# A metaformer kernel: token rows kept as fp16 halves and turned by transposing DMAs, a deeper split-ahead of the weights, and one product set for both embeddings

## What is computed

```
x = x + attention(ln_c(x))          # e1 = relu(w1 x + b1), e2 = relu(w2 x + b2), both with D = 64 channels
                                    # scores = e1^T e2, softmax; out = x attn; y = alpha * out + relu(w3 x + b3)
t = t + moe(ln_t(t))                # rmsnorm, router with 16 experts, top 4 of them per token
    gu = x @ gate_up_proj[e]        # (512 -> 2 * 1024), h = silu(gate) * up
    routed += aff * (h @ down_proj[e])   # (1024 -> 512)
    shared = (silu(x @ sgate) * (x @ sup)) @ sdown
x = x + scan(ln_c(x))               # 16 rows forward and back, one 512 x 512 matrix
t = t + ternary_ffn(ln_t(t))        # weights rounded to -1, 0, 1
```

## Time and profile before

| | before |
|---|---|
| median of 3 runs | 1105.28 us |
| lowest and highest | 1102.9 and 1105.73 us |
| the profiled execution's own time | 1101.8 us |
| span of its trace | 1100.1 us |
| mean granted TensorE clock | 0.957 of full speed |

### The profile page before, as it was taken

One profiled execution on the slowest core, in us unless ns is written; L12 is line 12 of the kernel. 1 busy time (PEld: TensorE's weight loads), 2 busy tenths in 40 slices (PEclk: granted clock), 3 DMA queues, 4 the chain that ended last, 5 costly groups with the idle time before them and its releaser, 6 DMA issues. The chain is left out here.

```text
span 1100.1 us, 21748 instructions
## 1 busy us (share of the span) xinstructions
PE 995.5 (90%) x8016; PEld 648.9 (59%) x8017; DVE 704.6 (64%) x1340; ACT 545.3 (50%) x898; POOL 150.1 (14%) x159
## 2 busy tenths in 40 slices
PE   5977499899899999999999999999998997985796
PEld 3434444367566666766667766766674446872453
DVE  5378896465666556576566665665764886658774
ACT  4623544255565455565555655565654413233674
POOL 0030001101011012011102210120112640002000
PEclk9998599899999999999999999999998998996998
DMA  8601134435656555556546764664567640000001
GB/s 304 232 1 38 40 131 161 140 115 189 217 186 207 171 176 200 176 199 215 186 142 225 234 209 149 238 219 168 204 229 224 194 114 1 1 0 0 1 20 57
DMA packets 116438, 162.68 MB, mean 148 GB/s; under 512 B 7569, under 2 KB 85393, under 8 KB 116402
## 3 DMA queue, kind: packets, MB, share of 16 engines
q1 hardware_dynamic: 104530, 130.30, 35.2%
q0 software_dynamic: 9168, 30.02, 8.1%
q10 hardware_dynamic: 2704, 1.87, 0.5%
HBM read 147.49 MB, written 14.68 MB: 147 GB/s over the span
## 5 line engine op out<-in xcount | busy, mean ns | idle before, releaser
L937 DVE SCALAR_TENSOR_TENSOR w_lo<-raw,w_hi 128x1024 f16<-128x1024 f32 x144 | 171.6, 1222 | 53.4 <-ACT w_hi L862 52.4
L1068 PE MATMUL gate_ps<-x_hi,w_hi 128*128 128x256 f16 (+2 forms) x576 | 173.0, 300 | 16.6 <-issue 7.3
L1069 PE MATMUL gate_ps<-x_lo,w_hi 128*128 128x256 f16 (+2 forms) x576 | 172.8, 300 | 0.0
L1070 PE MATMUL gate_ps<-x_hi,w_lo 128*128 128x256 f16 (+2 forms) x576 | 172.8, 300 | 0.0
L1068 PE MATMUL up_ps<-x_hi,w_hi 128*128 128x256 f16 (+2 forms) x576 | 171.0, 297 | 0.0
L1069 PE MATMUL up_ps<-x_lo,w_hi 128*128 128x256 f16 (+2 forms) x576 | 170.9, 297 | 0.0
L1070 PE MATMUL up_ps<-x_hi,w_lo 128*128 128x256 f16 (+2 forms) x576 | 170.9, 297 | 0.0
L862 ACT ACTIVATE w_hi<-raw 128x1024 f16<-128x1024 f32 x144 | 145.9, 1051 | 5.5 <-SPq L781 5.5
L868 ACT CAST h_hi<-hid 128x320 f16<-128x320 f32 (+1 forms) x144 | 68.5, 476 | 131.1 <-DVE hid L942 127.6
L866 ACT ACTIVATE gated<-gate_ps 128x320 f32<-128x320 f32 (+1 forms) x144 | 64.5, 448 | 133.1 <-PE up_ps L1070 133.1
L945 DVE TENSOR_TENSOR h_lo<-hid,h_hi 128x320 f16<-128x320 f32 (+1 forms) x144 | 74.2, 515 | 78.0 <-ACT h_hi L868 76.8
(11 more groups left out here) (255 smaller groups left out, 1575.6 us busy)
## 6 DMA issues: line engine op xcount, KB each, us to landing
raw<-in_gate_up SPq DMA_DIRECT2D x96, 512.0 KB, 4.3
raw_last<-in_gate_up SPq DMA_DIRECT2D x32, 512.0 KB
raw<-in_down SPq DMA_DIRECT2D x32, 512.0 KB, 5.4
raw_last<-in_down SPq DMA_DIRECT2D x32, 512.0 KB
weights<-in_f SPq DMA_DIRECT2D x3, 2816.0 KB, 16.3
slot_y<-y_sb POOLq DMA_DIRECT2D x16, 512.0 KB, 5.5
raw<-in_sgate SPq DMA_DIRECT2D x6, 512.0 KB, 4.9
raw<-in_sup SPq DMA_DIRECT2D x6, 512.0 KB, 5.9
```

The costliest lines, as they stand in the source:

```text
L937: V.scalar_tensor_tensor(w_lo[:, j % RING, c], raw[j % RING][:, c], W_SCALE, w_hi[:, j % RING, c], ALU.mult, ALU.subtract).then_inc(split_ ...
L1068: T.matmul(out, hi_a, hi_b, start=first, stop=False, **flags)
L1069: T.matmul(out, hi_a, lo_b, start=False, stop=False, **flags)
L1070: return T.matmul(out, lo_a, hi_b, start=False, stop=last, **flags)
```

## The change

Five things are changed.

1. **Both embeddings in one product set.** `reduce(n)` makes four products with all 128 columns of `w12`, into partitions 0 to 127 of `pe_`; `relu` reads e2 from partitions 64 to 127.
2. **Rows as fp16 halves.** `rows` holds all eight tiles, and the stores of `tokens` leave the attention stage. In unit 0, beside m = 3 to 6, ACT casts each tile to fp16 (`z_high`), DVE subtracts for the low half, and POOL stores both halves as one row of 1,024 fp16 values (2 KB, as before). `gather(0)` waits for all eight stores.
3. **Transposing DMAs.** The three gathers of an expert write `rows16`. SP then issues three DMAs with transpose (128 x 1024, 128 x 1024, 64 x 1024 fp16) straight into `x16`, whose first half is `x_hi` and second half `x_lo`. They stand behind the loads of pieces 0 and 1, wait until gate and up of the unit before are summed (`gu_summed`) and until the gathers have landed (`rows_in`), and the load of piece 2 stands behind them. For the last unit four such DMAs read the `tokens` in DRAM. PE waits on `x_in` where it waited on `x_lo_ready`. The transposes, the casts and the subtractions of the routed units and of the last unit are gone; unit 0 keeps them (`turn_first`).
4. **Five half pieces ahead.** Between two units ACT and DVE now split five halves: pieces 0 and 1 and the first half of piece 2 (`AHEAD = 5`). ACT makes the first two before `take_third`, the other three after it, the last of them (which waits on `y_summed`) in front of `take`. The last split of a unit moves from m = 7 to m = 6.
5. **Waits.** `gather(u)` waits for the transposes of the rows before (`x_in`) instead of PE's transposes. The wait for all eight rows of h (`h_ready`) at the end of d = 0 is gone; a wide unit has it in front of the third tile's second part.

```diff
                     pe.wait_ge(e_ready, 2 * n)
-                for j in range(2):
-                    for k in range(KC):
-                        mm = nc.tensor.matmul(pe_[0:D, j * SP:(j + 1) * SP], w12[:, k, j * D:(j + 1) * D],
-                                              xn_cm[:, k, n * SP:(n + 1) * SP], start=(k == 0), stop=(k == KC - 1))
+                for k in range(KC):
+                    mm = nc.tensor.matmul(pe_[:, 0:SP], w12[:, k, :], xn_cm[:, k, n * SP:(n + 1) * SP],
+                                          start=(k == 0), stop=(k == KC - 1))
                 mm.then_inc(e_summed, 1)
...
-        x_hi = sb("x_hi", [P, KC, HALF], F16)
-        x_lo = sb("x_lo", [P, KC, HALF], F16)
+        z16 = sb("z16", [P, Z_RING, 2, C], F16)
+        rows16 = sb("rows16", [P, UNIT_COLS, 2 * C], F16)
+        x16 = sb("x16", [P, 2 * KC, HALF], F16)
+        x_hi, x_lo = x16[:, 0:KC, :], x16[:, KC:2 * KC, :]
...
+        SPLIT_BESIDE = {3: (0, 1), 4: (2, 3), 5: (4, 5), 6: (6, 7)}
         MARK = NT * TOPK // MARKS
-        FIRST_HALVES = [(j, part) for j in range(2) for part in range(2)]
+        HALVES = [(j, part) for j in range(PIECES) for part in range(2)]
+        AHEAD = 5
...
+            def turn_rows(j, source, w):
+                sp.dma_start(x16[:, :, j * P:j * P + w], source, transpose=True).then_inc(x_in, 16)
...
-                    pieces(r * EXPERTS + e + 1, gu[:, :, 0:FF], gu[:, :, FF:2 * FF], dn, 0, PIECES)
+                    U = r * EXPERTS + e + 1
+                    sources = (gu[:, :, 0:FF], gu[:, :, FF:2 * FF], dn)
+                    pieces(U, *sources, 0, 2)
+                    sp.wait_ge(gu_summed, U * FH)
+                    sp.nop(nofuse=True)
+                    sp.wait_ge(rows_in, U * (16 * len(ROUTED)))
+                    sp.nop(nofuse=True)
+                    for j, w in enumerate(ROUTED):
+                        turn_rows(j, rows16[0:w, j, :], w)
+                    pieces(U, *sources, 2, PIECES)
             last = n * EXPERTS + 1
-            pieces(last, *shared, 0, RING)
-            sp.wait_ge(rows_turned, (last + 1) * KC)
-            sp.dma_start(rows[:, :, :], io["tokens"][HALF:TOK, :].rearrange("(j p) c -> p j c", p=P)).then_inc(shared_in, 16)
-            pieces(last, *shared, RING, PIECES)
+            pieces(last, *shared, 0, 2)
+            sp.wait_ge(gu_summed, last * FH)
+            sp.nop(nofuse=True)
+            for j, w in enumerate(SHARED):
+                turn_rows(j, io["tokens"][HALF + j * P:HALF + (j + 1) * P, :], w)
+            pieces(last, *shared, 2, PIECES)
 
...
-                pool.wait_ge(rows_turned, (u + 1) * KC)
+                pool.wait_ge(x_in, u * (16 * len(ROUTED)))
...
-                        out=rows[0:w, j, :], out_offset=None, in_=io["tokens"],
+                        out=rows16[0:w, j, :], out_offset=None, in_=io["tokens"],
...
+            for t in range(NT):
+                pool.wait_ge(z_ready, t + 1)
+                pool.dma_start(io["tokens"][t * P:(t + 1) * P, :],
+                               z16[:, t % Z_RING, :, :].rearrange("p h c -> p (h c)")).then_inc(tokens_out[t % Z_RING], 16)
+            for j in range(Z_RING):
+                pool.wait_ge(tokens_out[j], 16 * (NT // Z_RING))
             pool.wait_ge(listed, 1)
             gather(0)
...
+            def z_high(t):
+                if t >= Z_RING:
+                    act.wait_ge(tokens_out[t % Z_RING], 16 * (t // Z_RING))
+                S.copy(z16[:, t % Z_RING, 0, :], rows[:, t, :]).then_inc(z_hi_ready, 1)
+
+            def unit(U, n, beside=None):
+
+                for m in range(FH):
+                    hidden(U, m, n)
+                    if m + AHEAD < len(HALVES):
+                        hi(U, *HALVES[m + AHEAD])
+                    if beside:
+                        beside(m)
...
-            unit(0, HALF)
+            unit(0, HALF, lambda m: [z_high(t) for t in SPLIT_BESIDE.get(m, ())])
...
                 unit(u + 1, CAP)
-                turn(u + 2, CAP)
+                for j, part in HALVES[0:2]:
+                    hi(u + 2, j, part)
                 take_third(u)
-                for j, part in FIRST_HALVES:
+                for j, part in HALVES[2:AHEAD]:
                     hi(u + 2, j, part)
                 take(u)
...
+                for t in SPLIT_BESIDE.get(m, ()):
+                    dve.wait_ge(z_hi_ready, t + 1)
+                    V.tensor_tensor(z16[:, t % Z_RING, 1, :], rows[:, t, :], z16[:, t % Z_RING, 0, :],
+                                    ALU.subtract).then_inc(z_ready, 1)
...
-                    if d == 1 and next_rows and not (isinstance(U, int) and U == 0):
+                    if d == 1 and not last_unit and not (isinstance(U, int) and U == 0):
                         if wide:
+                            pe.wait_ge(h_ready, U * FH + FH)
...
-                        pe.wait_ge(h_ready, U * FH + FH)
-                        if next_rows:
-                            pe.wait_ge(*next_rows)
-                            turn(ROUTED)
-                    elif next_rows:
...
-                pe.wait_ge(x_lo_ready, (u + 2) * KC)
+                pe.wait_ge(x_in, (u + 1) * (16 * len(ROUTED)))
                 few = pe.value_load(narrow[0:1, bass.ds(u, 1)], min_val=0, max_val=1)
-                next_rows = (rows_in, (u + 2) * (16 * len(ROUTED)))
-
-
                 with pe.If(few > 0):
-                    unit(u + 1, tiles_of(NARROW), next_rows)
+                    unit(u + 1, tiles_of(NARROW))
                 with pe.Else():
-                    unit(u + 1, ROUTED, next_rows)
+                    unit(u + 1, ROUTED)
             last = n * EXPERTS + 1
-            pe.wait_ge(x_lo_ready, (last + 1) * KC)
-            pe.wait_ge(shared_in, 16)
-            turn(SHARED)
-            pe.wait_ge(x_lo_ready, (last + 2) * KC)
-            unit(last, SHARED, None)
+            pe.wait_ge(x_in, n * (EXPERTS * 16 * len(ROUTED)) + 16 * len(SHARED))
+            unit(last, SHARED, last_unit=True)
 
 
...
```

More of the change, by code:

```diff
@@ L903, in _ @@
             S.copy(bias_hi[:, :], bias).then_inc(conv_hi_ready, 1)
-            turn(1, CAP)
-            for j, part in FIRST_HALVES:
+            for j, part in HALVES[0:AHEAD]:
                 hi(1, j, part)
@@ L915, in _ @@
             last = n * EXPERTS + 1
-            turn(last + 1, HALF)
             unit(last, HALF)
```

69 lines of the change are left out of this document (30 added, 39 removed).

## The result

The changed kernel takes **1054.92 us** (median of 4 runs, 1050.92 to 1055.37), the kernel before, on the same chip in turn, 1104.09: a ratio of 0.9547, 95% interval 0.9531 to 0.9563. 1055.0 was predicted. The profiled execution took 1055.37 us, its span is 1053.8 against 1100.1.

The account below looks back on a forecast made before the run. PE's issue was taken to bound the expert loop, 600 us of the kernel. Terms -38.4 + 1 + 2 - 7.9 - 4.6 = -47.9 us from 1101.8 gave 1053.9, raised to a median of 1055 us; range 1046 to 1093.

Parts of the forecast that it names:

- part 1: Routed units: dropping the turn between d = 0 and d = 1, 17 times 2.26 us, takes 38.4 us off PE.
- part 4: ACT's fifth split before the copies of y fills idle time before silu; +1 us over narrow units, at most 8.
- part 5: Start of unit 1: the first gather waits for tile 7, so x comes later; +2 us, bounds 0 and 6.
- part 6: Last unit: the gap before it and slow first products shrink, -7.9 us; bringing back the results keeps up, zero.
- part 7: Attention stage: eight PE instructions per image, not sixteen, save 1.83 us on three images; -4.6 us, bounds 3.7 and 5.5.
- Part 2: Routed units: x arrives by transposing DMAs 7 us after gate and up, under the narrow window of 10.5; no cost.
- Part 3: SP's queue: piece 2, behind the three transposes, lands 6.6 us after gate and up, under 10.5 us; zero.
- The second rival: Wait on x_in replaces the turn: break-even at x 15 us after gate and up, 1182 us at 20; chance 0.17.

Follow-up runs that it names:

- alone: The kernel before with only the one product set for both embeddings, nothing else of the change: 1094.61 us, ratio 0.9930 to before.
- doubled transposes: The changed kernel with each routed unit's three transposing DMAs issued twice, first into a spare tile: 1073.09 us, ratio 0.9704 to 0.9737 to before.
- tripled kernel: The changed kernel with each transposing DMA issued three times, two of them into spare tiles: 1136.34 us, ratio 1.0276 to 1.0311 to before.

## Why the prediction was right

In the profiled executions 46.3 us went (1100.1 to 1053.8), 47.9 were forecast for that pair. Term by term:

| step of the prediction | forecast | measured |
|---|---|---|
| part 1, turns, with part 4, ACT's order | -38.4 + 1 | -39.1 (2.2 in unit 0, 8 x 2.28, 8 x 2.33) |
| part 5, unit 1 late | +2 | +1.6 (gap 4.77 to 5.82, and 0.5 inside unit 1) |
| part 6, last unit | -7.9 | -7.0 gap, -2.1 slow clock |
| part 7, product set | -4.6 | -1.9 here, -2.9 by the mean start of 133.2, -3.9 alone |
| the 2.52 us gap in the loop | none | -2.7 |
| end of the last unit | zero | +6.6 |
| scan and after | none | -1.7 |

**Part 1** held. Its risk, the narrow units, is settled by the turns put back: 2.25 us there too.

**Part 2** took 7 us for x to arrive; the trace has 5.7, and PE could start at 6.9. Its pieces were wrong against each other: SP's issue is 3.9 us, not 1.4, and 2.7 us of landing stand for the 5.6 that were taken. The estimate of some 4 us of SP, worked out from the Trainium skill's page "DMA: Bandwidth & Descriptors" (the table on the fast descriptor path), agrees with the trace's 3.91 in the sum. It does not in the parts: counted by tiles, the transpose of 64 rows would cost half of one of 128, and all of them take 1.24 to 1.34 us, so the trace bears out no price per tile. What I made of it there, a third piece too late by 1 us in each narrow unit, did not come. It comes with the next 4 us: the doubled transposes show it.

**Part 3** had the third piece land 6.6 us after gate and up. It lands at about 9.2, behind 3.9 us of transposes, still under the 10.4 us of a narrow unit.

**The second rival** ("the transposes become the bound") named the wait on x_in and t = 15 us as its turning point. The tripled kernel has x at 13.9 and PE's first product at 14.9, and is slower than before by 32 us. Waits for x alone give 41 us, close to the 47.9 of the rival's sum at t = 15. The clock behind each gap gives some 20 more; the rival named it and put no price on it. The waits for hid behind the third piece (11.6) and the start of unit 1 (8.1) give the other 20.

**Part 4** had the wrong sign and size. Silu did stay where it was, 2.8 us after the unit's first product, but the fifth half is no cost of 1 us; without it the narrow units lose 1.21 us each. Part 1 could count the whole 2.26 in narrow units only because of it.

**Part 5** had the size within 0.4 us and the cause, x, but not the rule that ties them. It had x arrive at 207 to 212, after PE is done with unit 0. Timelines of POOL, whose next gathers wait for x, and of ACT in the changed kernel:

```profile
205.17 0.18 POOL L818 COPY slot_ids<-lists 128x3 uint32 x1 [7.88 <-DMA x<-rows]
```

```profile
209.57 1.06 ACT L883 ACTIVATE w_hi<-raw_last 128x1024 f16<-128x1024 f32 x1 [10.95 <-DMA raw_last<-in_gate_up]
```

x was there by 205.2, 1.7 us before PE stopped at 206.9 (212.69 - 5.82). The profile names the low half of the third piece as what PE waited for. But with four halves ahead PE waits for no such half, and still stands 5.46 us. What fits all profiles is x. PE's first product of unit 1 comes 6.5 to 7.5 us after x has landed in eleven of the twelve profiles with transposing DMAs: at 212.7 after 205.2 in the change, 212.4 after 205.3 with four halves ahead, 215.4 after 208.2 doubled, 219.8 after 212.6 tripled. In the twelfth, with the turns on PE, PE is done later, and there it stands 4.6 us, as before the change (4.8). So unit 1 starts some 4.7 us behind the end of down or some 7 us behind x, whichever is later, and x should have been there 2.4 us before PE was done. Why this takes 7 us here and 1.1 us inside the loop was not followed.

**Part 7** counted three savings of 1.8 us. In the profile of the change the sums for images 1 and 2 show them, and that of image 0 none. In that profile the sums of image 1 also began 1.4 us later than before (34.30 against 32.87), inside the 2 us by which the start moves.

**Part 6 is the step that failed**: "it keeps up, and the first ones are a few us late for DVE, which PE waits for only two steps later. Zero." The gathers do keep their pace, one in 1.55 us, but they start with the last expert's store and not with PE, so the last of them comes late against PE by what they start late. What stands behind the last one on DVE, 7.8 us, lies bare as soon as PE is early. That cost 6.6 us, and part 7 brought 2.7 us less than forecast. The total came out right because the gap in the loop (2.7), the scan (1.7), 1.2 us more in part 6, 1.7 in parts 1 and 4 and 0.4 in part 5 gave 7.7 us the other way, 4.4 of it in no term of the sum. That the figure is this close (1055.0 against 1054.92) is luck. So is its last step: 1053.9 for the profiled execution was raised by 1.1 us to a median, while the kernel before's profiled execution lay 3.5 us under its median, and the change's, 1055.37, is the highest of its four.

## What to carry to other kernels

When a stage's last part gets a head start, look for what else must end there and is tied to the result before it, and move the work behind its last arrival to beside the arrivals: that gave some 5 us here for a few lines. A transfer that takes the place of engine work is safe by its window less its landing, and the loads queued behind it have a window of their own, which closed first here (the third piece lands at 9.2 us of 10.4, x at 5.7). Once such a wait opens it costs more than its length: here each 4.4 us of waiting were followed by some 4 us at 0.50 to 0.66 of the clock. The depth of a prefetch has a best value where the same engine also serves the short chain: four, five and six halves gave narrow units of 33.58, 32.37 and 33.63 us.

## What was not expected of the hardware

- A transposing DMA of 128 x 1024 fp16 holds SP for 1.3 us, one of 64 x 1024 as well, and a plain load of 512 KB for 0.4 to 0.5. Behind a weight load three took 5.2 us.
- 45,676 packets more (116,438 to 162,114), nearly all under 512 B, took the queue's share of the 16 engines from 35.2 to 41.0% and made no weight load late for PE in the routed units (a half piece of gate and up lands in 4.5 us, 4.3 before); the stores of y even landed in 3.2 us (5.5 before).
- A gather's issue on GpSimd lasts 0.95 us, and 2.15 beside a weight split on DVE.
- The gap of 2.52 us at the second narrow unit is in the profile of before alone. That it has to do with where code lies is a guess; nothing that ran tells.
